# A scan kernel's front, gate, skip and second layer norm one step later in all four items, and the copy of dt*x into PSUM in its own item's first step

## What is computed

```python
xn = layer_norm(xf, norm_g, norm_b)                 # over the 512 channels of a pixel
chunks = xn.reshape(B, L, 4, 128)...                # four groups of 128 channels: 4*B sequences of L = 4096
xi, z = split(einsum('bld,ed->ble', chunks, in_proj_w))        # 256 + 256
xc = silu(causal_conv4(xi) + conv_b)
dt, Bs, Cs = x_proj(xc)                             # 8, 16, 16
dt = softplus(dt @ dt_proj_w + dt_proj_b)
h = exp(dt * A) * h + (dt * xc) * Bs                # a scan over L, for each of 16 states
y = sum over states of h * Cs, + xc * D_param
ym = (y * silu(z)) @ out_proj_w + skip_scale * chunks
y = layer_norm(ym over 512 channels) @ proj_w + proj_b
```

## Time and profile before

| | us |
|---|---|
| median of 3 runs | 16086.48 (16082.97 to 16089.99) |
| the profiled execution | 16090.54 |
| its span | 16088.7 |
| DVE busy / POOL busy | 14823.6 / 14788.2 |
| PE busy / ACT busy | 14186.2 / 11509.9 |

### The profile page before, as it was taken

How to read it: one execution, slowest core, us unless ns; L and a number is a source line. 1 busy time by engine, 2 the same in 40 slices (tenths; PEclk the granted TensorE clock), 3 DMA queues, 4 the chain that set the end, 5 groups by cost and what they waited for, 6 DMA issues and landing times. The chain is left out here.

```text
span 16088.7 us, 151421 instructions
## 1 busy us (share of the span) xinstructions
PE 14186.2 (88%) x30720; PEld 5741.6 (36%) x30720; DVE 14823.6 (92%) x13024; ACT 11509.9 (72%) x18891; POOL 14788.2 (92%) x6275
## 2 busy tenths in 40 slices
PE   6988989889898898888889888899888898888888
PEld 2333333333333333333333333333333333333333
DVE  6999999999999999999999999999999999999998
ACT  5777767777677767777677776777767777677776
POOL 5999989999899989999899998999989999899998
PEclk8999999999999999999999999999999999999999
DMA  3444444444444444444444444444444444444444
GB/s 131 156 163 163 159 153 162 162 164 153 157 157 160 163 155 158 159 160 169 150 156 162 157 169 149 158 163 161 163 148 161 164 160 166 150 153 164 156 154 139
DMA packets 739082, 2537.63 MB, mean 158 GB/s; under 512 B 77241, under 2 KB 78017, under 8 KB 721729
## 3 DMA queue, kind: packets, MB, share of 16 engines
q1 hardware_dynamic: 738112, 2527.45, 46.1%
HBM read 2376.15 MB, written 150.99 MB: 157 GB/s over the span
## 5 line engine op out<-in xcount | busy, mean ns | idle before, releaser
L1460 POOL TENSOR_TENSOR RING<-RING,CS 128x1024 f32<-128x1024 f32 x4096 | 9597.9, 2363 | 1036.2 <-DVE RING L1150 973.3
L1150 DVE TENSOR_TENSOR_SCAN RING<-DA,HS,RING 128x512 f32<-128x512 f32 x8192 | 9946.1, 1265 | 496.9 <-ACT DA L777 451.1
L388 PE MATMUL YP<-RING,EYE 128*128 128x512 f32 x16384 | 8172.0, 632 | 1400.6 <-POOL RING L1460 1307.3
L777 ACT ACTIVATE DA<-ITEM,AN 128x512 f32<-128x512 f32 x8192 | 5495.8, 684 | 3017.5 <-DVE RING L1150 3001.5
L388 PEld LDWEIGHTS YP<-RING,EYE 128*128 128x128 f32 x16384 | 3126.8, 198 | 5995.0 <-issue 3596.3
L1130 DVE TENSOR_TENSOR RING<-DTP,BS 128x1024 f32<-128x1024 f32 x3072 | 3687.7, 1205 | 129.0 <-ACT DTP L847 117.6
L1447 POOL TENSOR_TENSOR RING<-ITEM,BS 128x1024 f32<-128x1024 f32 x1024 | 2421.3, 2365 | 10.0 <-DMA BS<-bc_rows 0.3
L388 PE MATMUL FL<-XN,WC 128*128 128x512 f32 x4096 | 1913.9, 611 | 9.8 <-ACT XN L866 4.6
L388 PEld LDWEIGHTS FL<-XN,WC 128*128 128x128 f32 x4096 | 821.4, 201 | 1087.4 <-issue 1079.1
L791 ACT ACTIVATE ITEM<-FL,COL 128x512 f32<-128x512 f32 x512 | 348.9, 682 | 1056.8 <-PE FL L388 1056.6
L388 PE MATMUL FL<-LS,WP 128*128 128x512 f32 x2048 | 983.2, 603 | 6.1 <-POOL LS L1482 6.1
(11 more groups left out here) (125 smaller groups left out, 10879.3 us busy)
## 6 DMA issues: line engine op xcount, KB each, us to landing
BS<-bc_rows SPq DMA_DIRECT2D x2048, 512.0 KB, 4.9
CS<-bc_rows SPq DMA_DIRECT2D x2048, 512.0 KB, 3.6
XR<-in_x SPq DMA_DIRECT2D x128, 1024.0 KB, 7.6
x_slices<-XR SPq DMA_DIRECT2D x64, 1024.0 KB, 8.3
XR<-x_slices SPq DMA_DIRECT2D x64, 1024.0 KB, 7.6
out<-XR SPq DMA_DIRECT2D x64, 1024.0 KB, 8.1
XR<-in_wqkv SPq DMA_DIRECT2D x24, 1024.0 KB, 7.8
bc_rows<-ROWS SPq DMA_DIRECT2D x256, 64.0 KB, 4.5
```

Source lines behind the costliest of these rows:

```text
L388: return pe.matmul(*a, **k)
L777: act.activation(DA[:, h, :], DT[:, i % 2, h, :], ACT.Exp, scale=AN[:, h, s:s + 1]).then_inc(dA_ready, 1)
L1150: dve.tensor_tensor_scan(H[:, slot(n), h, :], DA[:, h, :], U[:, slot(n), h, :], HS[:, i % ITEMS, h, s:s + 1], ALU.mult, ALU.add).then_inc( ...
L1460: pool.tensor_tensor(G[:, slot(n)], H[:, slot(n)], CS[:, s % C_ROWS, :].unsqueeze(1).broadcast_to([P, NH, T]), ALU.mult).then_inc(g_ready, 1)
```

## The change

`late()` returns 1 for every item, and the new `conv_late()` keeps `xi_first` where it was. So for items 0, 1 and 2 `xi_second`, z, dbc, dt_proj, out_proj, the ACT and POOL work of the front, the gate, add_skip and the first layer norm's steps stand one step later. Of the second layer norm the first two channel means, the centring, proj(0) and finish(0) move by one step. `dtx_copy` moves from step 15 to step 0 of its item's own window, behind DA(0), and U1 to step 1, behind scan 0.

```diff
-AHEAD_LATE = ((1,), (2,), (3,), (4,), (5,), (7,), ...
+AHEAD_LATE = ((), (1, 2,), (3,), (4,), (5,), (7,), ...
...
         def late(j, new=False):
-            return 1 if j == 3 or new else 0
+            return 1
+        def conv_late(j, new=False):
+            return j == 3 or new
...
                     if front:
-                        if s == 0 and d:
+                        if s == 0 and conv_late(j, new):
                             front_left(tile, w)
...
                     if j == 0 and ln2:
-                        if s == 7:
+                        if s == 8:
                             pe.wait_ge(yb_ready, tile * ITEMS + w)
                             channel_mean(YB, mu2_ready, (0, 1))
-                        if s == 8:
+                        if s == 9:
                             channel_mean(YB, mu2_ready, (2, 3))
...
                     if j == 1 and ln2:
-                        if s == 6:
+                        if s == 7:
                             pe.wait_ge(yn_ready, ahead)
                             pe.wait_ge(yb_ready, tile * ITEMS + w)
                             proj(0, (0, 1))
-                        if s == 7:
+                        if s == 8:
                             proj(0, (2, 3))
...
-                    if front and s == 15:
-                        dtx_copy(tile, w + 1)
+                    if s == 0 and not first:
+                        dtx_copy(tile, w)
...
-                    if j == 0 and ln2 and s == 9:
+                    if j == 0 and ln2 and s == 10:
                         centre(YB, mu2_ready, cen2_ready, ahead)
                     if j == 1 and ln2:
-                        for at, o in ((8, 0), (11, 1), (13, 2), (15, 3)):
+                        for at, o in ((9, 0), (11, 1), (13, 2), (15, 3)):
```

More of the change, by code:

```diff
@@ L47 @@
 AHEAD = ((1,), (2,), (3,), (4,), (5, 7,), (), (), (9,), (), (11,), (12,), (13,), (14,), (15,), (), ())
-AHEAD_LATE = ((1,), (2,), (3,), (4,), (5,), (7,), (), (9,), (), (11,), (12,), (13,), (14,), (15,), (), ())
+AHEAD_LATE = ((), (1, 2,), (3,), (4,), (5,), (7,), (), (9,), (), (11,), (12,), (13,), (14,), (15,), (), ())
 def block_ssm_kernel(nc, x, wqkv, bq, bk, bv, norm_g, norm_b, w_in, conv_w, conv_b, w_x, w_dt, dt_b,
```

## The result

The changed kernel takes **16579.02 us** (median of 4 runs, 16574.99 to 16583.4) against 16084.72 us for the kernel before beside it (4 runs, 16072.48 to 16089.99): ratio **1.0308, 95% interval 1.0291 to 1.0326**. It is slower, as forecast, but by 494 us and not by 124: outside the range. The profiled execution took 16574.99 us, its span 16573.2.

A forecast was written before the change was run, and what follows sets the result against it. DVE and POOL waiting for each other bound the kernel, each window a loop of two legs. Item 2 +1.9, item 0 +1.2 and item 1's credits a window summed to +124 us: 16210 us (+0.8%), range 16045 to 16320.

The forecast's parts named there:

- the exchange of waits: DVE's gate wait goes to near zero; scans wait for DA instead, some 300 us more than 451.
- Faster: the gate's wait was the loop's: Rival: the gate's wait goes, POOL's gaps before G3 and G4 close, nothing replaces them; 15870 or 15980 us; chance 0.16.
- the chain of 6.7 us: From gate's end through state_sum(0), z, silu, table load and DA(5); some 2.1 us of waiting for DA(5).
- the walk: Step-by-step timing of item 0's window: scan 5 at 62.4 against 61.70, U of step 0 ending 1.2 us later.
- the burst's shift: POOL's dt operations one step later, dt_first behind G10: up to 1.2 us later, 0 where POOL isn't waiting.
- POOL has no gap in the regular window, nor will it: +0.1: Item 1's regular window: POOL stays without a gap, so the window grows by only 0.1 us.
- +2 a tile if not: Bound for item 1: PE idle before the late gate costs 2 us a tile (130 us) unless its backlog clears before G15.
- passes the delay on, 0 of its own: Item 3's front doesn't move; its later wait for DA takes up scan 0's later start, adding 0.
- The credits: Gains in windows with slice statistics or attention: item 1 with statistics about 2 us each, item 0 with attention 1.5.
- -1.5: Item 0 with attention: 1.2 us longer, less the extra gate wait of 4.82 - 2.16.
- lies beside scan 0 and costs nothing: The 1.0 us dt*x copy on ACT costs nothing; if cover were gone, up to 1.0 a window.
- dearer: Rival: ACT's crowding or PE's backlog in item 1 real in each tile, +3 to +5 us a tile; 16320 to 16450; chance 0.09.

The follow-up runs named there:

- e2_z_first: The changed kernel with the z projection back in step 2, ahead of state_sum(0): 16177.32 us, ratio 1.0063.
- e8_dt_first: The changed kernel with z ahead of state_sum(0), dtx copy and U1 back, scaling in step 14, dt_first in step 9: 16015.78 us, ratio 0.996.
- e1_fill: The changed kernel with three unused matmuls added on PE behind the conv projection of items 0 to 2: 16430.54 us, ratio 1.0221.
- e5_scale_back: The changed kernel with the first layer norm's scaling back in step 14 of item 2's window: 16575.65 us, ratio 1.0308.
- e11_centre_back: e8_dt_first with item 0's centring back in step 9 and the four channel means together in step 8: 15995.38 us, ratio 0.9939.
- e4_dtx_back: The changed kernel with the dt*x copy back in step 15 and U1 back ahead of scan 0: 16384.32 us, ratio 1.0189.

## Why the prediction was right or wrong

**Right: the direction and the exchange of waits.** The gate's wait went (473.2 to under 5 us) and scan 5's wait for DA took its place, over state_sum(0), z, silu and table load. e2_z_first takes z out of that chain and scan 5's wait falls to 0.44 us. "Faster: the gate's wait was the loop's" was wrong for a regular tile; it holds for the windows with statistics, where e8_dt_first keeps that gain.

**The term that failed most: the chain of 6.7 us, "state_sum 1.7 and z 1.9".** Measured from the gate's end it is 8.6 us (5297.93 to 5306.56; the five terms as given add up to 6.6). Silu, table and DA came as forecast (5303.49 to 5306.56, 3.1 against 3.0); state_sum(0) and z took 5.4 and not 3.6. The durations had been read where PE was busy just before. The prediction had seen that PE "stands idle about 2 us before the late gate", but asked only whether its backlog would be worked off. Idle for 3.15 us, PE came back at a granted clock of 0.81 and 0.59. e1_fill shows that this is the cause: with the idle stretch filled, the chain is 6.9 and the wait 2.31. So the chain was the right one, with the clock behind the new idle stretch left out of its two PE terms. Taking z out of it is worth 402 us in all, the clock's share among them (e2_z_first).

Two rules of the Trainium skill bear on this chain. "TensorE: Matmul & The Clock Gate", section "Part 1: The HAM clock gate", says that half clock is the default of TensorE and activity releases it; the trace agrees as far as 0.52 to 0.81 after 3.1 us without matmuls, with the tile that kept 1.00 beside it. The 2.66 us a table switch of "ScalarE: Activation LUTs", section "What ACT_TABLE_LOAD costs", are not seen after the change either: load and DA start 1.29 apart (5304.54 and 5305.83).

**Item 0** came out at +4.35 instead of +1.2. Scan 5 starts 26.39 us after U of step 0, 23.46 before: +2.9 where the walk had +0.7, 1.9 of it the chain. From scan 5 to the window's end it is 1.4 us more than before where the walk had 0.5: DVE takes 12.8 us from scan 5 to scan 9 and not 12.2, and POOL waits before G9, G10 and G11 (1.18, 1.17, 0.98). The order of z is worth 3.4 us of this window, the clock's 1.7 among them (62.90 to 59.47), U1's place another 0.6 (58.85). dt_first behind G10, the walk's reason for the burst's shift, is worth nothing in item 0: e8_dt_first takes it back and the window stays at 58.85.

**Item 1**, "POOL has no gap in the regular window, nor will it: +0.1", was +2.2. 1.7 of it is the clock again (e1_fill: 60.79), and with z first the window is at 60.38, the forecast +0.1. The bound "+2 a tile if not" was of the right size by luck: it stood for a backlog of PE, but e1_fill gives PE more work in this window and shortens it. The reason for +0.1 (POOL full) holds only while DVE's leg is shorter; after the change POOL waits 1.80 us before G10.

**Item 2** was right in a regular tile: +2.1 measured, +1.9 forecast, and G10 starts 45.8 us after U of step 0, as in the walk; it is the window in which the clock stayed full.

**Item 3**, "passes the delay on, 0 of its own", was +1.5. That scan 0 waits for ACT's normalisation, as forecast, doesn't carry it: it starts 3.40 us behind U of step 0 (5467.86 to 5471.26) and started 4.15 behind before, where U1 was made first, and e5_scale_back takes the wait away with the window still at 64.89. The delay comes over PE, whose clock is down here too. PE in item 3, before and after:

```profile
5322.01 1.98 PE L388 MATMUL YP<-RING,EYE 128*128 128x512 f32 x4 [2.65 <-POOL RING L1460]
5326.15 3.60 PE L388 MATMUL FL<-XN,WC 128*128 128x512 f32 x8
...
5472.57 5.83 PE L392 MATMUL YP<-RING,EYE 128*128 128x512 f32 x8 [3.32 <-POOL RING L1464]
5478.24 3.60 PE L392 MATMUL FL<-XN,WC 128*128 128x512 f32 x8
```

```profile
5473.00:5478.00 5.00, 5.00 (x8) 1.99 (x8) 5.00 (x5) 2.64 (x5) 5.00 (x3) 0.61 0.61 210
```

Two state_sums lasted 5.83 us at a granted clock of 0.61, so the conv projection starts 10.4 us after U of step 0 and not 8.9, and scan 5, which waits for it over ACT, 27.9 and not 26.4. In all 28 regular tiles of both kernels the window is 54.5 us longer than the time to that start, within 0.02: item 3 is set by it. No run fills this idle stretch, so the clock's part is read from the trace alone.

**The credits.** The credit of 2 us for an item 1 with slice statistics was right: the two windows of an image went from 64.74 and 64.53 us to 62.73 and 62.29. But the item 2 behind each grew from 61.89 and 66.56 to 66.05 and 71.22, by 4.2 and 4.7 us instead of 1.9, and took it back. I had given these windows a credit on POOL's leg and no price on DVE's. It is z behind the gate again: PE stands idle for 5.2 us before state_sum(0) there, and e2_z_first has 62.33 and 69.2 us. The item 0 with attention, "-1.5", was +2.4 (62.21 to 64.57): the extra wait at the gate went, but the step moved for the centring probably costs more there: undone in e11_centre_back, together with the means', it gives this window 3.4 us back from e8_dt_first.

**The copy of dt\*x** "lies beside scan 0 and costs nothing": U1's move cost 195 us as the kernel stood, some of it by the clock, and 68 once z was back. The removed wait of 117.6 us was worth less than the cover it came with.

**The range** was too narrow for one reason: each of these terms is a delay on the same leg, and once DVE's leg sets every window, all of them count in full. The "dearer" rival had PE's backlog in item 1 as one of its two causes, but no clock; its own 5 us a tile on top of 16210 would have been 16530 and not the 16450 at which it stopped. By item, the sum missed 183, 76, 51 and 43 us.

## What to carry to other kernels

Before moving a consumer later, ask what the producer will do in the gap: work that stands behind the wait in its queue and doesn't need it (here z) belongs ahead of it, both to cover the wait and to keep TensorE busy. Cost a matmul behind a new idle stretch at either level of the clock and carry both into the range. An operation that moves costs what it covered, and two delays on one leg are not measured by undoing one: undo them singly, together, and in the kernel before.

## What the runs showed of the hardware

The price of a short idle stretch on TensorE was not expected: after 3.1 us without matmuls in an otherwise dense stream, four fp32 products of 128x512 (eight matmuls in the trace) took 5.4 us instead of 3.6, at a granted clock of 0.81 and 0.59, and 148 us of 16579 (0.9%) came back with useless matmuls in the gap. It isn't the same each time: with 3.14 us idle one tile kept 1.00 and a later one of the same run fell to 0.66, and an item 2 with 2.83 us of idle time kept 1.00, while an item 0 of the last image with 2.82 us (until 15802.46) had its state_sum(0) take 3.54 us, and an item 1 of e4_dtx_back with 2.25 us (until 5311.28) had it take 3.33. So the length of the stretch alone doesn't tell it. The whole run's clock moved only from 0.947 to 0.932, so it doesn't stand out on the page; the stretch behind the wait has to be looked at.
